# A transformer block on one core: the token part and the cross-attention in one tile-by-tile phase

## The reference

```python
def block_forward(x, codebook_embeds, codebook_mask, ...):
    xn = layer_norm(x, ln0_w, ln0_b)
    q, k, v = ...                              # heads of xn @ qkv_w.T
    attn = softmax(einsum('bhnd,bhmd->bhnm', q, k) * SCALE)
    x = x + merge(einsum('bhnm,bhmd->bhnd', attn, v)) @ sa_proj_w.T
    xn = layer_norm(x, ln1_w, ln1_b)
    q = heads(xn @ q_w.T)
    k = heads(codebook_embeds @ k_w.T)
    v = heads(codebook_embeds @ v_w.T)
    attn = softmax(einsum('bhnd,bhmd->bhnm', q, k) * SCALE + bias)
    x = x + merge(einsum('bhnm,bhmd->bhnd', attn, v)) @ ca_proj_w.T
    xn = layer_norm(x, ln2_w, ln2_b)
    return x + (gelu(xn @ fc1_w.T + fc1_b) @ fc2_w.T + fc2_b)
```

## Time and profile before

| what | value |
|---|---|
| median of three runs | 3851.54 us |
| the profiled execution | 3855.14 us |
| its span, first to last instruction | 3853.4 us |
| mean granted TensorE clock | 0.899 |
| TensorE busy | 3510.2 us (91%) |
| VectorE busy | 2233.3 us (58%) |
| ScalarE busy | 1597.1 us (41%) |
| GpSimd busy | 1702.5 us (44%) |

### The profile page before, as it was taken

The page is one execution under the profiler, slowest core; times in us unless marked ns, Lnnn a source line. Parts: engine busy times, 40 slices in busy tenths (PEclk is TensorE's granted clock), DMA queues, the critical chain, the costliest instruction groups (busy, mean ns, idle before and its releaser), DMA issues. The chain is left out here.

```text
span 3853.4 us, 53748 instructions
## 1 busy us (share of the span) xinstructions
PE 3510.2 (91%) x16392; PEld 2134.2 (55%) x16392; DVE 2233.3 (58%) x3777; ACT 1597.1 (41%) x2855; POOL 1702.5 (44%) x510
## 2 busy tenths in 40 slices
PE   7998999999999999999996698599996869999999
PEld 6884444444444444444442476343433648888887
DVE  4446788888888888888882344345543842222222
ACT  3221666666666666666665232133343331111111
POOL 0001888887888888888887121233233200000000
PEclk9996999999999999999998799555556989999999
DMA  4546446574646546474434444766542762111110
GB/s 164 186 161 156 100 88 132 108 154 87 133 99 135 120 92 133 104 154 99 100 79 114 142 175 172 156 139 127 124 95 101 274 211 74 44 44 44 44 44 22
DMA packets 184386, 455.68 MB, mean 118 GB/s; under 512 B 23218, under 2 KB 47560, under 8 KB 158588
## 3 DMA queue, kind: packets, MB, share of 16 engines
q1 hardware_dynamic: 163708, 318.26, 28.9%
q0 software_dynamic: 18432, 134.23, 17.3%
q10 hardware_dynamic: 2048, 0.53, 0.1%
HBM read 198.35 MB, written 119.34 MB: 82 GB/s over the span
## 5 line engine op out<-in xcount | busy, mean ns | idle before, releaser
L1597 DVE TENSOR_REDUCE self_part_max<-self_first 128x1 f32<-128x512 f32 x2048 | 1279.0, 676 | 305.5 <-PE self_first L1454 302.3
L1555 ACT ACTIVATE self_expo<-self_second 128x512 f32<-128x512 f32 x2048 | 1068.5, 602 | 696.2 <-PE self_second L1470 664.1
L1403 POOL TENSOR_TENSOR self_pair_sum<-self_expo 128x2048 f32<-128x2048 f32 x192 | 883.3, 4601 | 115.6 <-ACT self_expo L1555 89.6
L1454 PE MATMUL self_first<-self_k,self_q 96*128 96x512 f32 x2048 | 887.8, 441 | 42.1 <-DVE self_part_max L1597 24.4
L1470 PE MATMUL self_second<-self_q,self_k 98*128 98x512 f32 x2048 | 816.0, 402 | 13.4 <-ACT self_expo L1555 13.3
L1454 PEld LDWEIGHTS self_first<-self_k,self_q 96*128 96x128 f32 x2048 | 396.3, 194 | 561.5 <-DVE self_part_max L1597 440.3
L1483 PE MATMUL self_weighted<-self_expo,self_v_sb 128*32 128x512 f32 x4096 | 547.5, 606 | 8.9 <-ACT self_unscaled L1567 6.7
L1470 PEld LDWEIGHTS self_second<-self_q,self_k 98*128 98x128 f32 x2048 | 390.2, 191 | 109.5 <-ACT self_expo L1555 47.0
L1949 DVE CAST mlp_h_high<-mlp_h 128x512 fp32r<-128x512 f32 x128 | 54.9, 429 | 506.9 <-PE mlp_out_sum L61 506.9
L1924 ACT ACTIVATE mlp_h<-mlp_hidden_sum,mlp_b_col 128x512 f32<-128x512 f32 x128 | 88.3, 690 | 603.1 <-PE mlp_hidden_sum L61 603.1
L1403 POOL TENSOR_TENSOR self_half_sum<-self_expo 128x2048 f32<-128x2048 f32 x64 | 292.9, 4582 | 88.4 <-ACT self_expo L1555 88.4
(11 more groups left out here) (166 smaller groups left out, 4337.5 us busy)
## 6 DMA issues: line engine op xcount, KB each, us to landing
self_half_sum<-self_pair_sum POOLq DMA_DIRECT2D x128, 1024.0 KB, 7.2
self_k<-k_t SPq DMA_DIRECT2D x96, 256.0 KB
cross_q_hold<-cq_t SPq DMA_DIRECT2D x24, 1024.0 KB, 12.2
cross_q_move<-cq_t SPq DMA_DIRECT2D x24, 1024.0 KB, 14.2
self_q<-q_t SPq DMA_DIRECT2D x93, 256.0 KB, 4.6
qkv_x<-in_x SPq DMA_DIRECT2D x8, 1024.0 KB, 5.9
v<-qkv_v_sb SPq DMA_DIRECT2D x32, 256.0 KB, 2.0
q_t<-qkv_r_high SPq DMA_DIRECT2D x32, 256.0 KB, 2.0
```

Of the source, the lines that this page charges most:

```text
L1403: nc.gpsimd.tensor_tensor(to, expo[:, t % p_slots], expo[:, (t + 1) % p_slots], ALU.add).then_inc(pair_done, 1)
L1454: nc.tensor.matmul(first[:, in_ring[n]], q[0:base, c % q_slots, a, s * P:(s + 1) * P], k[0:base, c // stages_per_group % 2, a, k0:k0 + TOK ...
L1555: nc.scalar.activation(expo[:, t % p_slots, a], second[:, n % ring], ACT.Exp, scale=scale).then_inc(exp_done, 1)
L1597: nc.vector.tensor_reduce(part_max[:, a * SUB + s, k:k + 1], first[:, in_ring[n]], AX_X, ALU.max).then_inc(first_read, 1)
```

## The change

`mid` and `cross` become one phase, `cross_phase`; `order_of_work` and `attention_phase` go, and `self`, `context`, `late` and `mlp` stay as they are. The new phase goes through the 8 tiles of 512 tokens in straight-line code. While tile t is in its second pass, TensorE turns tile t+1 and multiplies out its queries, then projects three quarters of tile t+2, then does the first pass of all 16 heads of t+1 with the last quarter of the projection between. Keys, values and mask rows of both batches are loaded once. There is one buffer of x, one of stacked queries `q`, and `xn` lies in the buffer of the loaded attention output. PSUM has three banks for all dense products and transposes, four for scores (the first pass uses them in two pairs, a pair per head; the second pass three of them, `weigh` the fourth) and one for `total`.

The queries don't go to DRAM: when the high and low part of a group of four heads are there, SP copies them with 12 DMAs of 64 KB from `r_high` and `r_low` (two slots) into `q` (`stack_q`). The maxima are sent in two halves, by ScalarE's queue. The norm's weight is multiplied into the query weights when these are split, and its bias becomes a bias of the queries, made once by 16 one-column products; a turned chunk is then read once by ScalarE, and VectorE takes the low part from PSUM. The division inverts `total` where it lies in PSUM, in four pieces.

The diff, cut to what sets the order; of what is left out, removed lines too, nothing is marked but by the dots:

```diff
-def order_of_work(steps, heads, n_parts, products, sums, sum_ends, p_slots, ring, parts, first_steps, item_cost):
...
-def attention_phase(nc, name, q_t, k_t, v, out, keys, tiles_per_stage, mask_rows=None):
...
+def cross_phase(nc, name, x_in, attn, proj_w, ln_w, ln_b, q_w, k_t, v, mask_rows, x_out, out):
...
+    pair_slots = 2
+    r_slots = 2
+    s_ring = 3
+    d_ring = 3
+    pieces = 4
...
+                def stack_q(t, g):
+                    ge(sp, r_ready, groups * t + g + 1)
+                    ge(sp, second_done, n_seconds * (t - 1) + per_group * (g + 1))
+                    for j, src in enumerate((r_high, r_low, r_high)):
+                        for a in range(heads):
+                            sp.dma_start(q[j * HEAD_DIM:(j + 1) * HEAD_DIM, heads * g + a].bitcast(F32),
+                                         src[a * HEAD_DIM:(a + 1) * HEAD_DIM, g % r_slots].bitcast(F32)).then_inc(
+                                q_loaded[g], 16)
...
+                def period(t):
+                    if t + 2 < tiles:
+                        load_attn(t + 2)
+                        load_x(t + 2)
+                    for g in range(groups):
+                        if g == 1 and t > 0:
+                            store_out(t - 1, groups - 1)
+                        if g > 1:
+                            store_out(t, g - 2)
+                        if t + 1 < tiles:
+                            stack_q(t + 1, g)
+                    store_out(t, groups - 2)
+                    if t + 2 < tiles:
+                        store_x(t + 2)
...
+                def turn(t, c):
+                    if c == 0:
+                        pe.wait_ge(xn_ready, SUB * (t + 1))
+                    to = dense_free(("turn", t, c))
+                    for s in range(SUB):
+                        mm = nc.tensor.transpose(to[:, s * P:(s + 1) * P], xn[:, s, c * P:(c + 1) * P], identity[:])
+                    mm.then_inc(turn_done, 1)
...
+                def first_pass(t, h):
+                    b, u = t // tiles_per_batch, 2 * (h % 2)
+                    if h % heads == 0:
+                        pe.wait_ge(q_loaded[h // heads], 16 * 3 * heads * (t + 1))
+                    if h == 0:
+                        if t == 0:
+                            pe.wait_ge(k_loaded, 64 * batches)
+                            pe.wait_ge(rows_set, 2)
+                        ge(pe, exp_done, n_seconds * t)
+                    if h == 1:
+                        ge(pe, weighted_read, groups * t)
+                    if h >= 2:
+                        pe.wait_ge(first_read, n_heads * t + h - 1)
+                    for s in range(SUB):
+                        mm = nc.tensor.matmul(score[:, u + s // 2, s % 2 * keys:(s % 2 + 1) * keys],
+                                              q[0:score_rows, h, s * P:(s + 1) * P], k[0:score_rows, b, h],
                                               start=True, stop=True)
+                    mm.then_inc(first_done, 1)
...
+                def second_pass(t, n):
+                    g, kt, a = n // per_group, n // heads % n_k, n % heads
+                    h = heads * g + a
+                    b = t // tiles_per_batch
                     if n == 0:
+                        pe.wait_ge(first_read, n_heads * (t + 1))
+                    if n % (n_seconds // halves) == 0:
+                        pe.wait_ge(max_loaded[n // (n_seconds // halves)], 32 * (t + 1))
+                    if n >= s_ring:
+                        pe.wait_ge(exp_done, n_seconds * t + n - s_ring + 1)
+                    nc.tensor.matmul(score[0:width, n % s_ring], k[0:exp_rows, b, h, kt * width:(kt + 1) * width],
+                                     q[0:exp_rows, h], start=True, stop=True).then_inc(second_done, 1)
...
+                def add_up(t, g):
+                    n = groups * t + g
+                    ge(pe, mean_done, n)
+                    pe.wait_ge(pair_done, n + 1)
                     for a in range(heads):
+                        rows = slice(a * HEAD_DIM, (a + 1) * HEAD_DIM)
+                        mm = nc.tensor.matmul(total[rows], ones[0:width], pair_sum[0:width, g % pair_slots, a],
+                                              start=True, stop=True)
                     mm.then_inc(total_done, 1)
...
+                def firsts(t, project_last):
+                    for h in range(n_heads):
+                        first_pass(t, h)
+                        if project_last and h < 12:
+                            some(project_last, 1)
+                        if h == half_heads + 1:
+                            turn_max(t, 0)
+                    turn_max(t, 1)
...
+                def groups_of(t, g):
+                    if g > 0:
+                        for kt in range(n_k):
+                            weigh(t, g - 1, kt)
+                    if g == 1 and t > 0:
+                        add_up(t - 1, groups - 1)
+                    if g > 1:
+                        add_up(t, g - 2)
...
+                def period(t):
+                    has_next, has_after = t + 1 < tiles, t + 2 < tiles
+                    for g in range(groups):
+                        work = result(t + 1, g - 1) if g > 0 and has_next else iter(())
+                        for n in range(per_group):
+                            second_pass(t, g * per_group + n)
+                            if g == 0 and has_next and n % 2 == 1:
+                                turn(t + 1, n // 2)
+                            if n == 2:
+                                groups_of(t, g)
+                            if n >= 2:
+                                some(work, 2)
+                    if has_next:
+                        rest(result(t + 1, groups - 1))
+                    groups_of(t, groups)
+                    if has_after:
+                        for s in range(SUB - 1):
+                            rest(project(t + 2, s))
+                    if has_next:
+                        firsts(t + 1, project(t + 2, SUB - 1) if has_after else None)
...
+                def take_weighted(t, g):
+                    n = groups * t + g
+                    act.wait_ge(weighted_done, n_k * (n + 1))
                     ge(act, mean_done, n)
+                    nc.scalar.activation(unscaled[:], weighted, ACT.Copy).then_inc(weighted_read, 1)
...
+                def period(t):
+                    has_next = t + 1 < tiles
+                    for g in range(groups):
+                        for n in range(per_group):
+                            exponential(t, g * per_group + n)
+                            if g == 0 and has_next and n % 2 == 1:
+                                high_turned(t + 1, n // 2)
+                            if n == 5 and g > 0:
+                                take_weighted(t, g - 1)
+                            if n == per_group - 1 and g > 0 and has_next:
+                                high_result(t + 1, g - 1)
+                        if g == 1 and t + 2 < tiles:
+                            high_attn(t + 2)
+                    if has_next:
+                        high_result(t + 1, groups - 1)
+                    take_weighted(t, groups - 1)
+                    if has_next:
+                        for half in range(halves):
+                            send_max(t + 1, half)
...
+                def maxima(t, h):
+                    u = 2 * (h % 2)
+                    dve.wait_ge(first_done, n_heads * t + h + 1)
+                    if h == 0:
+                        ge(dve, max_turned, halves * t)
+                    nc.vector.tensor_reduce(
+                        row_max[:, h * SUB:(h + 1) * SUB].rearrange("p (b s) -> p b s", s=2),
+                        score[:, u:u + 2, 0:2 * keys].rearrange("p b (s k) -> p b s k", k=keys),
+                        AX_X, ALU.max).then_inc(first_read, 1)
...
+                def divide(t, g):
+                    n = groups * t + g
+                    dve.wait_ge(total_done, n + 1)
+                    for part in range(pieces):
+                        cols = slice(part * (TOK // pieces), (part + 1) * (TOK // pieces))
+                        nc.vector.reciprocal(total[:, cols], total[:, cols]).then_inc(inverse_done, 1)
+                    dve.wait_ge(inverse_done, pieces * (n + 1))
+                    dve.wait_ge(weighted_read, n + 1)
+                    ge(dve, out_stored[g % 2], 16 * (n // 2))
+                    nc.vector.tensor_tensor(mean[:, g % 2], total[:], unscaled[:], ALU.mult).then_inc(mean_done, 1)
...
+                def firsts(t, after):
+                    for h in range(n_heads):
+                        maxima(t, h)
+                        if after is not None:
+                            if h == 11:
+                                add_projection(after, SUB - 1)
+                                stats_of(after, SUB - 1)
+                                for s in range(SUB):
+                                    moments_of(after, s)
```

(29 more changed lines are left out.)

931 lines of the change are left out of this document (394 added, 537 removed).

## The result

The changed kernel took 3684.55 us (median of four runs, 3680.09 to 3685.76), the kernel before beside it 3850.47 us: a ratio of 0.9565, 95% interval 0.9549 to 0.9582. The forecast was 3743 with a range of 3670 to 3840. The profiled execution took 3683.99 us with a span of 3682.2.

The account below looks back on a forecast made before the run. TensorE at the low clock was taken as the bound, with fills on top. Prologue, six periods, a period without projection and the last tile summed to 678 us against 787.8, a gain of 109: 3743 us, range 3670 to 3840.

Parts of the forecast that it names:

- rival W: Fused stage: the clock survives the first pass; period 67.7 us, stage 611 us, kernel 3675 us; chance 0.12.
- (g): Prologue of the fused stage, up to the last maximum of tile 0: 98 us.
- (a): From a tile's last `add_up` (T0) to the next tile's last maximum (T1): clock falls after four heads; 30.4 us.
- (b): Group 0: `turn` waits for `norm`, 3.4 us, then eight exponentials with four turned copies, 6.9; together 10.3 us.
- (c): Group 1 starts at the low clock, which rises during some 8 us of unbroken full products: 13 us.
- (d): Groups 2 and 3, high clock: a loop through the division sets group 2's 9.5 us; group 3 takes 12.5.
- (h): Stage total: prologue 98, six periods 454, one without projection 65, last tile 61; 678 us against 787.8.
- Rival M: Second pass: the clock comes back a group later, groups 1 and 2 at 14.8 us, +7.1 per period; 3793; chance 0.20.
- (e): On-chip query stacking: 48 DMAs per tile take 22 us of SP, hidden; landing 2.5 us; only the prologue pays.
- rival S: Stacking queue: small DMAs don't overlap, 2.0 us each; period 100 us, slower, 3997; chance 0.07.
- (f): Folded norm weights: 32 ScalarE copies go, nothing more on the path; 16 bias products add 4 us once.
- Rival C: Fused period: clock isn't won back before the next dense end; 102 us, 3941; decides from 87 us; chance 0.07.

## Why the prediction was right, and where it was off

The sign was right and the range held the time, but only because it took in rival W: the time is near that of W (3675), to which I gave 0.12, and not near the forecast. The sum for the stage was 678 us; 621.4 were measured. By its steps, for an undisturbed period:

| step | predicted | measured |
|---|---|---|
| (g) prologue | 98 | 98.4 |
| (a) T0 to T1 | 30.4 | 25.3 |
| (b) norm and group 0 | 10.3 | 9.4 |
| (c) group 1 | 13 | 9.1 |
| (d) group 2 | 9.5 | 9.1 |
| (d) end | 12.5 | 12.4 |
| period | 75.7 | 65.4 |
| six periods | 454 | 401.7 |
| (h) period 6, last tile | 65, 61 | 61.1, 60.3 |

The prologue's 98.4 is partly luck, since the same instructions took 103.1 us in the other profile of this kernel. The step that failed is the clock, in (a) and (c), and the six periods hold 52 of the 57 us.

In (a) I let the clock fall after four heads, because 328 to 360 us of the kernel before shows first-pass products alone at 0.50. That was a weak reading: there the clock was at 0.50 already, behind 12.8 us in which TensorE waited for a load, so the stretch shows only that it didn't rise, not that it falls. For a first pass without anything mixed in the conclusion was right all the same: that kernel loses the clock every time. But here one full product follows each of twelve heads, and the clock read 1.00 up to the last 3 to 4 us in four of the six first passes that have one; the one without lost it. I had named this as what speaks for W and gave it too little. Where the clock was lost, the first pass took 20.4 and 20.6 us instead of 16.9, 1.28 a head against my 1.37 at the low clock.

In (c) I let it come back in the middle of group 1, behind unbroken full products. It came back in group 0 already, about 7 us behind the last maximum, among second products and the transposes of `turn`. Rival M said that such narrow products wouldn't do it; the last tile with narrow ones shows that they can. (Its 14.8 us for a group at the low clock doesn't come out of its own terms, 5.6 + 20 x 0.43 = 14.2.)

(d) was right in its size and its cause: two buffers removed the wait and brought the group to the 7.6 us that the sum gives without the loop. (e) was right that the transfers are hidden and overlap; the landing was 2.0 us against 2.5. Its issue was too small: 0.62 us each, not 0.45, so 48 take 30 us; and "10 us and more to spare" was wrong, since in a group hardly any is left. The rule cited with rival S, that under 64 KB one pays mostly overhead (the Trainium skill, "DMA: Bandwidth & Descriptors", section "Rules for kernel authors"), shows here as a landing of 2.0 us and 0.62 us of the issuing queue for each; the landings overlap, so it is the queue that runs out. In (f) and (b) I left out four copies of 0.6 us a tile; given back as reads they cost 1.0 us a tile, not 2.4. Maxima took 0.794 us (0.78 taken), reciprocals 0.919 (0.95).

Rival C had nearly the right threshold. It said that from a period of 87 us on the change is worth nothing; the kernel with its results behind the groups has 92 us and took 3867, from which about 90 follows. So the whole gain hung on one property of the order of instructions, and the forecast's chance of 0.07 for losing it was a judgement on this order alone.

Open remain: what exactly makes the clock fall in a period in which nothing else differs (tile 0 at 69.5 and 61.9 us in two executions), what makes it fall in group 3, and how large the part of the clock alone is, apart from the idle time that the results fill and the transfers that they spread.

## What to carry to other kernels

When one phase has full-size products and another leaves TensorE waiting at the low clock, interleave them product by product: here that was worth 183 us against the same fused phases with the full products in one block, which gained nothing; part of the 183 us is transfers that came in a burst. Before calling an interleaving a matter of the clock, see what else the block form delays. Cost a period at both clocks and give both a real chance; a stretch of the trace speaks only for the same mixture of products. Compare the issuing queue with the shortest interval in which its transfers come, not with the whole period, and give each value that two engines hand on in a loop two buffers before looking for anything finer.

## What the runs showed of the hardware

- TensorE was busy for 225.84 of 234 us and its granted clock stayed at 0.50; a high busy share did not bring the high clock. The same ten 512-column products in a row raised it in one stage and left it at 0.50 in five others.
- The clock fell to 0.50 for some 5 us in a stretch in which TensorE shows 7.00 of 7 us busy.
- Products without use made a stretch shorter: 48 more of them, and the last tile fell from 60.3 to 51.7 us (55.2 with narrow ones).
- The same instructions (the period of tile 0) took 61.9 and 69.5 us in two executions, and the prologue ahead of them 103.1 and 98.4.
- Copies of 64 KB within the chip landed 2.0 us after their issue and overlapped; each took 0.62 us of the issuing queue, so that thirteen issues fitted between two groups 9.1 us apart and twenty-one did not.
